# A macaron block on one core: the heads' outputs of three rounds stored and reloaded instead of turned, the preparation reordered, and a new table of ticks

## The chip, the cores and the metric

The kernel runs on one core of a Trainium2 chip. The metric is the device time of one execution in microseconds (us). In the profile PE is TensorE, DVE is VectorE, ACT is ScalarE, POOL is GpSimd and SP is SyncE, which here only issues DMAs.

## What is computed

The input x is 16 batches of 512 rows of 128 numbers. The block is half a feed-forward, attention, half a feed-forward, each added to x:

```python
    x = x + 0.5 * _L0_ffn_ref(_layernorm(x, axis=-1), L0_ffn_weight, L0_ffn_bias)
    x = x + _L0_attn_ref(_layernorm(x, axis=-1), L0_attn_Wq, ..., L0_attn_temperature)
    x = x + 0.5 * _L0_ffn_ref(_layernorm(x, axis=-1), L0_ffn_weight, L0_ffn_bias)
```

The feed-forward is one 128x128 product with a bias, of which both the input and the weight are first rounded to a six-bit grid, with a scale for each block of 32. Attention has 16 heads of 8 dimensions:

```python
        scores = jnp.einsum('bhqd,bhkd->bhqk', Q, K) / scale
        mask = _tpms_mask(L, phase, threshold, temperature)
        scores = scores + TPMS_WEIGHT * jnp.log(mask + 1e-06)[None]
        attn = jax.nn.softmax(scores, axis=-1)
        out = jnp.einsum('bhqk,bhkd->bhqd', attn, V)
        out = out.transpose(0, 2, 1, 3).reshape(B, L, H)
        return out @ Wo + bo
```

The mask depends on the head and not on the batch: a sigmoid of sines and cosines of the two positions.

## The kernel before

Four batches make a **round** (`NQ = 4` rounds of `QB = 4` batches); attention of a round is a **period**. A period is 16 heads, and each head has 8 **ticks** (`STEPS`), two for each batch, so a period has 128 ticks and the kernel 64 heads, numbered m = 0 to 63 here (head 34 is the third head of the third period).

**A tick.** PE makes two blocks of scores (line 1614, 128x512 each) into one of two halves of S_PS; ACT takes the exponential of the 128x1024 result (line 738). In every odd tick PE also makes one of four products of the previous head's exponentials with the values (line 1628, "weighted values"), with a column of ones, so that row 8 of each batch's 32 rows holds the sum. The scores are accumulated on a seed: for the first batch of a head DVE copies the head's logarithmic mask into S_PS (line 1212, four copies of 128x512, the "seeds"). The seeds of a half can only be written when the exponential before has read that half, so between the last exponentials of a head and the first of the next there is a **seam**: exponential of tick 6, two seed copies, scores, exponential of tick 0, and beside it the exponential of tick 7, two more copies, scores of tick 1. A new seed for the later batches is not needed, since the products accumulate differences from one batch to the next.

**The end of a head.** `o_copy` (ACT, line 747) copies O_PS to OTS at the start of the head two later. `turn_o` (PE, line 1637) transposes it in four pieces into R_PS in tick 1, and `o_norm` (DVE, lines 1225 and 1227) divides by the sums and writes the head's 8 columns of AT. After 16 heads the epilogue of the round runs during the next period: for each batch `turn_at` (PE, line 1510), `at_copy` (ACT, line 675), `out_product` (PE, line 1515 with WO), `add_attention` (DVE, 1236), statistics, the rounding to the grid (`centre`, `block_tops`, `block_scales`, `to_grid`, `from_grid`), and per batch `turn_xd1`, `xd_copy1`, `ffn1`, `add_ffn`. The epilogue of the last round stands alone at the end.

**What sets the order.** Each engine's program is written out by hand. `attention(q)` runs through the ticks of a period, and `background(q, tick)` puts the other work (the first feed-forward of later rounds, the chain of projections and splittings into three bfloat16 parts of the next round, the bounds, the epilogue of the previous round) at the ticks that tables name: FIRST, LATE, CHAINS with SECOND, and LAST. In ticks 0 and 1 of a head PE does its background before the tick's scores, in ticks 2 to 7 behind them. In LAST of before the grid of a round is worked in one call over four batches for rounds 0 to 2 and in two calls for the last (`calls_of`).

**The parts of Q and K** are stored in DRAM (q_parts, k_parts) and loaded for each head as a "stack" of six DMAs and a seventh of shift rows (`load_stack`, `load_shift`); the mask of a head is a load of 1 MB (`load_mask`). SP issues all of these in `head(m)`, in program order, in one queue: mask of m+1, stack of m+1, shift of m+1, then stores.

**The preparation** (before the first exponential) makes the sines, the mask of all 16 heads in two halves (`val` on PE, line 1801, 32 tiles; `sigmoid`, line 779, and `ln_mask`, line 786, on ACT), the first feed-forward of round 0, and its projections, with POOL storing the parts. From tile 6 of the first half the factors are stacked three times in the partitions (`COPIES`, `FIRST_COPIED`), and PE waits for those loads.

Of the kernel before, what the change touches and what calls it, by code (L numbers as in the profile page):

```python
# [8 lines left out]
ALU = mybir.AluOpType  # L9
# [20 lines left out]


# [11 lines left out]
K_LOADS = 16 * (2 * len(GROUPS) + 1)  # L43

# [33 lines left out]
FIRST = dict(stats_ve=(0, 2, 4, 8), centre_ve=9, lnexp_act=10, rstd_ve=12, reduce_ve=14, scales_ve=16,  # L78
             to_grid_ve=17, from_grid_ve=19, turn_pe=(22, 24, 28, 32), xd_copy_act=(22, 24, 28, 32),
             ffn_pe=(24, 27, 31, 35), add_ve=(25, 28, 32, 36), stats1_ve=(27, 29, 33, 37), lnexp1_act=(31, 39),  # L80
             rstd1_ve=(33, 41), norm_ve=(41, 57, 73, 89))


LATE = ((dict(stats_ve=(50, 52), lnexp_act=54, rstd_ve=60, centre_ve=64, reduce_ve=66, scales_ve=68, to_grid_ve=72,
              from_grid_ve=74, turn_pe=(82, 90), xd_copy_act=(82, 90), ffn_pe=(84, 92), add_ve=(85, 93),
              stats1_ve=(88, 96), lnexp1_act=98, rstd1_ve=99),
         dict(stats_ve=(82, 83), lnexp_act=87, rstd_ve=91, centre_ve=97, reduce_ve=98, scales_ve=101, to_grid_ve=104,
              from_grid_ve=106, turn_pe=(110, 118), xd_copy_act=(110, 118), ffn_pe=(112, 120), add_ve=(113, 121),
              stats1_ve=(114, 122), lnexp1_act=124, rstd1_ve=125)),
        (dict(stats_ve=(26, 28), lnexp_act=30, rstd_ve=32, centre_ve=33, reduce_ve=34, scales_ve=36, to_grid_ve=41,  # L90
              from_grid_ve=44, turn_pe=(50, 58), xd_copy_act=(50, 58), ffn_pe=(52, 60), add_ve=(53, 61),
              stats1_ve=(57, 66), lnexp1_act=69, rstd1_ve=73),
         dict(stats_ve=(76, 81), lnexp_act=83, rstd_ve=84, centre_ve=90, reduce_ve=91, scales_ve=92, to_grid_ve=97,
# [21 lines left out]
def macaron_kernel(nc, x, Wq, bq, Wk, bk, Wv, bv, Wo, bo, phase, threshold, temperature,  # L115
                   w_ffn, b_ffn, pos, out):
    with ExitStack() as ctx:
# [57 lines left out]
        def stage(h):  # L175
            return big(2048 * STAGE[h], 2048)
# [128 lines left out]
        def first_bank(n, j):  # L305
            return F_PS if n in (2, 3) else (P_PS, F_PS)[j % 2]
# [1585 lines left out]
```

## Time and profile before

| | us |
|---|---|
| median of 3 runs | 877.73 (876.89 to 878.03) |
| the profiled execution: its time | 877.97 |
| the profiled execution: first to last instruction | 876.0 |
| preparation, to the first exponential | 139.0 |
| periods 0, 1, 2, 3 | 179.3, 177.4, 174.0, 160.4 |
| last epilogue | 46.0 |

The profiled execution takes 1.97 us more than its span, and its time is 0.24 us above the median. All stretches are read from the span's start. A period is from the first exponential of its first head to that of the next period; the fourth ends when the last exponentials do.

### The profile page before, as it was taken

How to read it: one execution, taken by the hardware profiler on the slowest of the kernel's cores; microseconds unless marked ns; L12 is line 12 of the kernel's file. 1: busy time of each engine (PE TensorE's matmuls, PEld its weight loads, DVE VectorE, ACT ScalarE, POOL GpSimd, SP SyncE). 2: the span in 40 equal slices, each digit the busy share in tenths (PEclk: the TensorE clock that was granted, in tenths of full speed). 3: DMA queues.
4: the chain of work that ended last, by engine and by line, in shares of the span. 5: the costliest groups of instructions: out<-in, count | busy, mean ns of one | idle time of the engine just before them, and what ended most of it. 6: DMA issues, size and time to landing. Idle time of an engine off the chain costs nothing.

```text
span 876.0 us, 13047 instructions
## 1 busy us (share of the span) xinstructions
PE 738.6 (84%) x4355; PEld 259.7 (30%) x4355; DVE 556.2 (63%) x1464; ACT 669.2 (76%) x799; POOL 191.0 (22%) x164
## 2 busy tenths in 40 slices
PE   0376626999999999999999999999999998999844
PEld 0043311232333323333333234223321331331234
DVE  8866573866889756899784456885433457432265
ACT  1379654888888788888888888888888887888811
POOL 0305750202353203163240031341200002000011
PEclk9987755999999999999999999999999999999987
DMA  5529497865666674756867538668676555456101
GB/s 148 121 77 370 174 314 248 254 209 160 200 207 198 196 222 138 221 185 165 248 191 231 180 114 234 204 170 247 200 225 186 173 173 173 150 192 208 42 1 53
DMA packets 56071, 162.11 MB, mean 185 GB/s; under 512 B 14121, under 2 KB 24497, under 8 KB 45579
## 3 DMA queue, kind: packets, MB, share of 16 engines
q1 hardware_dynamic: 51740, 154.36, 57.4%
q0 software_dynamic: 1808, 5.94, 2.1%
q10 hardware_dynamic: 2446, 0.89, 0.5%
q8 instruction: 37, 0.61, 0.3%
q14 instruction: 40, 0.32, 0.1%
HBM read 117.87 MB, written 43.29 MB: 184 GB/s over the span
## 4 chain that ended last, share of the span: by engine, by line
PE 53%; DVE 20%; ACT 10%; issue 8%; DMA 6%; POOL 2%; SPq 1%; ACTq 0%; DVEq 0%; POOLq 0%
PE S_PS L1614 19%; PE O_PS L1628 18%; ACT BIG L738 9%; DVE S_PS L1212 5%; PE F_PS L1515 4%; PE R_PS L1637 3%; PE F_PS L1510 2%; DMA PART<-trig_parts 2%; DMA k_parts<-PART 2%; PE P_PS L1552 1%; DVE PART L1114 1%; PE P_PS L1515 1%; DVE SC L1053 1%; DVE XC L1098 1%; DVE BIG L1043 1%
## 5 line engine op out<-in xcount | busy, mean ns | idle before, releaser
L738 ACT ACTIVATE BIG<-S_PS 128x1024 f32<-128x1024 f32 x512 | 508.5, 1023 | 109.9 <-PE S_PS L1614 107.6
L1614 PE MATMUL S_PS<-BIG 98*128 98x512 bf16 x1024 | 311.3, 389 | 37.4 <-DMA BIG<-shift_rows 13.7
L1212 DVE COPY S_PS<-BIG 128x512 f32<-128x512 f32 x256 | 159.6, 687 | 180.7 <-ACT BIG L738 178.5
L1628 PE MATMUL O_PS<-BIG,VX 128*9 128x512 f32 x2048 | 268.4, 597 | 1.2 <-ACT OTS L747 1.2
L1614 PEld LDWEIGHTS S_PS<-BIG 98*128 98x128 bf16 x1024 | 79.2, 98 | 290.7 <-ACT BIG L738 136.1
L572 POOL TENSOR_TENSOR XDT<-PART 128x512 bf16<-128x512 f32 x24 | 28.8, 1201 | 292.9 <-ACT PART L706 292.9
L1628 PEld LDWEIGHTS O_PS<-BIG,VX 128*9 128x9 f32 x2048 | 30.8, 88 | 103.4 <-issue 98.7
L549 POOL TENSOR_TENSOR X<-X,BFH 128x512 f32<-128x512 f32 x16 | 24.0, 1521 | 155.2 <-DVE BIG L1043 120.2
L588 POOL TENSOR_TENSOR PART<-PART 128x512 bf16<-128x512 f32 x32 | 41.5, 1297 | 38.5 <-DVE PART L1120 38.5
L581 POOL TENSOR_TENSOR PART<-PART 128x512 f32<-128x512 f32 x32 | 39.6, 1239 | 42.6 <-DVE PART L1114 41.2
L779 ACT ACTIVATE BIG<-S_PS,TEMP 128x1024 f32<-128x1024 f32 x32 | 34.4, 1111 | 18.1 <-PE S_PS L1801 17.6
L549 POOL TENSOR_TENSOR BIG<-BIG,BFH 128x512 f32<-128x512 f32 x16 | 19.9, 1272 | 127.8 <-DVE BIG L1043 111.8
L747 ACT ACTIVATE OTS<-O_PS,CON 128x512 f32<-128x512 f32 x64 | 44.0, 688 | 4.4 <-PE R_PS L1637 4.4
L1637 PE MATMUL R_PS<-IDENT,OTS 128*128 128x128 f32 x256 | 40.3, 280 | 1.8 <-ACT OTS L747 1.8
L675 ACT ACTIVATE XDT<-F_PS 128x512 f32<-128x512 f32 x38 | 22.6, 594 | 18.5 <-PE F_PS L1510 18.5
L1637 PEld LDWEIGHTS R_PS<-IDENT,OTS 128*128 128x128 f32 x256 | 27.7, 142 | 18.2 <-issue 15.0
L1515 PE MATMUL F_PS<-WDT,XDT 128*128 128x128 f32 x208 | 31.0, 295 | 0.0
L1515 PEld LDWEIGHTS F_PS<-WDT,XDT 128*128 128x128 f32 x208 | 27.1, 200 | 12.8 <-ACT XDT L675 7.3
L786 ACT ACTIVATE BIG<-BIG,CON 128x2048 f32<-128x2048 f32 x16 | 30.7, 1987 | 0.0
L1510 PE MATMUL F_PS<-IDENT,BIG 128*128 128x128 f32 x112 | 17.9, 284 | 14.0 <-DVE BIG L1079 10.2
L1114 DVE CAST PART<-PART 128x512 bf16<-128x512 f32 x32 | 22.9, 717 | 10.1 <-ACT PART L706 4.5
L1225 DVE RECIPROCAL RD<-R_PS 128x16 f32<-128x16 f32 x64 | 16.3, 255 | 18.0 <-PE R_PS L1637 17.5
(190 smaller groups left out, 737.8 us busy)
## 6 DMA issues: line engine op xcount, KB each, us to landing
BIG<-ln_masks SPq DMA_DIRECT2D x62, 1024.0 KB, 6.3
ln_masks<-BIG SPq DMA_DIRECT2D x16, 1024.0 KB, 7.1
BIG<-q_parts SPq DMA_DIRECT2D x63, 192.0 KB
BIG<-k_parts SPq DMA_DIRECT2D x63, 144.0 KB
BIG<-q_parts SPq DMA_DIRECT2D x63, 128.0 KB
q_parts<-PART SPq DMA_DIRECT2D x9, 768.0 KB, 3.8
k_parts<-PART SPq DMA_DIRECT2D x18, 384.0 KB, 4.7
BIG<-k_parts SPq DMA_DIRECT2D x63, 96.0 KB
```

What stands on the lines that cost most here:

```text
L549: pool.tensor_tensor(Y, Y, bias[:, None, :].to_broadcast((128, T, H)), ALU.add).then_inc(s[name], 1)
L581: pool.tensor_tensor(F_, F_, hi, ALU.subtract).then_inc(s[f"{q}_r1"], 1)
L588: pool.tensor_tensor(P_[2], F_, P_[1], ALU.subtract).then_inc(s[f"{q}_lo"], 1)
L738: act.activation(E[:, m % 2, j, 2 * pair:2 * pair + 2, :], S_PS[:, pair, :, :], ACT.Exp, scale=LOG_WEIGHT)\
L747: act.activation(OTS[:, :], O_PS[:, :], ACT.Identity, bias=CON[:, 2:3]).then_inc(s["o_copied"], 1)
L779: act.activation(stage(h)[:, 1024 * pair:1024 * pair + 1024].rearrange("p (k l) -> p k l", l=L), S_PS[:, t % 2, :, :], ACT.Sigmoid, scale= ...
L1212: ve.tensor_copy(S_PS[:, pair, i, :], LNM[:, slot, 2 * pair + i, :]).then_inc(s["seeded"], 1)
L1510: mm = pe.transpose(dst[:, 128 * t:128 * t + 128], src[:, t, :], IDENT[:, :])
L1515: mm = pe.matmul(dst[:, 128 * t:128 * t + 128], lhsT[:, 128 * t:128 * t + 128], rhs[:, :], start=True, stop=True)
L1614: mm = pe.matmul(S_PS[:, pair, i, :], KT[0:ALL_ROWS, slot, K_COL[j], 128 * kb:128 * kb + 128], QT[0:ALL_ROWS, slot, j, :], start=False, st ...
L1628: mm = pe.matmul(O_PS[32 * j:32 * j + HD + 1, :], VX[:, slot_of(n), j, kb, h, :], E[:, m % 2, j, kb, :], start=kb == 0, stop=kb == T - 1)
L1637: mm = pe.transpose(R_PS[:, 128 * t:128 * t + 128], OTS[:, 128 * t:128 * t + 128], IDENT[:, :])
```

## The change

- **Outputs by way of DRAM** (rounds 0 to 2, `BY_DRAM = 3`). `turn_o`, `o_norm`, `turn_at` and `at_copy` are left out for heads 0 to 47. SP stores each head's OTS (256 KB) to DRAM (`store_o`, new tensor head_rows), in `head(m)` between the load of the mask and the load of the stack. `o_copy` now waits for the store of the head before (`o_out`) where it waited for the transpose. In the next period the sums of all 16 heads are loaded (`load_sums`), inverted by DVE in one instruction of 128x256 (`invert`), stored and loaded again so that each stands on the 8 partitions of its head (`store_inverses`, `load_inverses`, 1 MB), and the rows are loaded already turned (`load_rows`, 1 MB). DVE multiplies each batch's 128x512 (`normalize`, four for a round), and `out_product` uses that directly. Heads 48 to 63 go the old way.
- **The ticks**: all tables are new. The grid of the epilogue is worked in two calls in every round. More of PE's products stand in ticks 0, 1 and 6.
- **The preparation**: the weight's grid is worked behind the grid of x on DVE, on another tile (WG); PE makes 8 tiles of the mask, then turns the first two batches; tiles up to 11 of the first half are taken with the single copy of the factors (`FIRST_COPIED = (12, 2)`). The parts of odd batches have buffers of their own (QPN_ODD, KP_ODD, in the room of stored masks). POOL adds the output bias of round 0 behind the loads of the first stack. The shift rows of head 0 are copied within SBUF by four small DMAs as soon as they are there; the store to DRAM that they took before follows. On ACT the first bounds stand behind the 11th logarithm instead of the 14th.

The diff, cut to its core:

```diff
+BY_DRAM = NQ - 1
+FIRST_TURNED = NH * BY_DRAM
...
-COPIES, FIRST_COPIED = 3, (6, 2)
+COPIES, FIRST_COPIED = 3, (12, 2)
...
-LAST = ({}, AMID, AMID, ALONE)
+LAST = ({},
+        dict(invert_ve=19, normalize_ve=(42, 45, 50, 57), out_pe=(48, 57, 65, 73), add_ve=(48, 56, 64, 72),
...
+            def store_o(m):
+                n, h = m // NH, head_of(m)
+                sp.wait_ge(s["o_copied"], m + 1)
+                if n >= 2:
+                    sp.wait_ge(s["rows_in"], 16 * (n - 1))
+                sp.dma_start(O_D[n % 2, h].rearrange("r j l -> j r l"), OTS[:, :]).then_inc(s["o_out"], 16)
+
+            def load_sums(n):
+                sp.wait_ge(s["o_out"], 16 * NH * (n + 1))
...
+            def load_rows(n):
+                sp.dma_start(ROWS.rearrange("p j l -> p (j l)"),
+                             O_D[n % 2, :, 0:HD].rearrange("h d j l -> h d (j l)")).then_inc(s["rows_in"], 16)
...
             def head(m):
                 q, i = m // NH, m % NH
                 more = m + 1 < NQ * NH
+                if q > 0:
+                    if i == SUMS_HEAD:
+                        load_sums(q - 1)
+                    if i == SUMS_HEAD + 1:
+                        store_inverses(q - 1)
                 if more and m >= 1:
                     load_mask(m + 1)
+                if q > 0 and i == SUMS_HEAD + 1:
+                    load_rows(q - 1)
+                if q > 0 and i == SUMS_HEAD + 2:
+                    load_inverses(q - 1)
+                if 2 <= m < FIRST_TURNED + 2:
+                    store_o(m - 2)
+                if more and m >= 1:
...
             def o_copy(m):
                 act.wait_ge(s["pv_done"], T * (m + 1))
-                if past(m):
-                    act.wait_ge(s["o_turned"], m)
+                if m > FIRST_TURNED:
+                    act.wait_ge(s["o_turned"], m - FIRST_TURNED)
+                elif past(m):
+                    act.wait_ge(s["o_out"], 16 * m)
...
             pool.wait_ge(s["bound_copied"], 1)
+            for t in range(T):
+                pool.dma_start(QT[QK_ROWS:ALL_ROWS, 0, :, 128 * t:128 * t + 128],
+                               CB4[T * head_of(0) + t:T * head_of(0) + t + 1, :, :, :]).then_inc(s["first_stack"], 16)
             pool.dma_start(SHIFT_D[0].rearrange("e j h (t l) -> (h t) (e j) l", t=T),
                            CB4.rearrange("p e j l -> p (e j) l")).then_inc(s["first_out_shift"], 16)
-            load_shift(pool, 0)
...
+            def normalize(n, j):
+                ve.wait_ge(s["rows_in"], 16 * (n + 1))
+                ve.wait_ge(s["inverse_in"], 16 * (n + 1))
+                TT(ROWS[:, j, :], ROWS[:, j, :], INV[:, j, :], ALU.mult).then_inc(s["at_ready"], 1)
...
-                    if k == 1 and m >= 2:
...
+                    if k == 1 and m >= FIRST_TURNED + 2:
                         turn_o(m - 2)
```

What the change does to the order is seen at three places. The first is PE in head 34 (third head of the third period), here before, from the scores of tick 0 to those of tick 5. S_PS is a score, O_PS the weighted values, R_PS<-IDENT,OTS `turn_o`, F_PS<-IDENT,BIG `turn_at`, F_PS<-WO,XDT `out_product`, the others the chain of the next round:

```order
L1614 MATMUL S_PS<-BIG 128x512 x2
L1637 MATMUL R_PS<-IDENT,OTS 128x128 x4
L1614 MATMUL S_PS<-BIG 128x512 x2
L1628 MATMUL O_PS<-BIG,VX 9x512 x4
L1614 MATMUL S_PS<-BIG 128x512 x2
L1510 MATMUL F_PS<-IDENT,BIG 128x128 x4
L1614 MATMUL S_PS<-BIG 128x512 x2
L1628 MATMUL O_PS<-BIG,VX 9x512 x4
L1614 MATMUL S_PS<-BIG 128x512 x2
L1575 MATMUL R_PS<-XDT,HSEL 16x512
L1515 MATMUL F_PS<-WO,XDT 128x128 x4
L1614 MATMUL S_PS<-BIG 128x512 x2
```

and after, the same ticks (the four score matmuls of ticks 0 and 1 now stand in a row):

```order
L1758 MATMUL S_PS<-BIG 128x512 x4
L1772 MATMUL O_PS<-BIG,VX 9x512 x4
L1758 MATMUL S_PS<-BIG 128x512 x2
L1721 MATMUL R_PS<-XDT,HSEL 16x512
L1758 MATMUL S_PS<-BIG 128x512 x2
L1772 MATMUL O_PS<-BIG,VX 9x512 x4
L1758 MATMUL S_PS<-BIG 128x512 x2
L1729 MATMUL R_PS<-HSEL,XDT 128x16 x4
L1731 MATMUL R_PS<-KDIAG,ONES 128x16
L1758 MATMUL S_PS<-BIG 128x512 x2
```

The transposes of OTS and of AT are gone, and the output product has moved to a later head (four heads later for the first batch), into tick 0 or 1.

The second place is SP in one head of the second half of the third period, before (a mask, then the stack and shift rows of the next head):

```order
L421 DMA BIG<-ln_masks 128x2048
L361 DMA BIG<-k_parts 48x1536
L364 DMA BIG<-q_parts 48x2048
L361 DMA BIG<-k_parts 32x1x1536
L364 DMA BIG<-q_parts 32x1x2048
L361 DMA BIG<-k_parts 16x1x1536
L364 DMA BIG<-q_parts 16x1x2048
L374 DMA BIG<-shift_rows 2x4x512
```

and after:

```order
L430 DMA BIG<-q_parts 48x2048
L427 DMA BIG<-k_parts 32x1x1536
L430 DMA BIG<-q_parts 32x1x2048
L427 DMA BIG<-k_parts 16x1x1536
L430 DMA BIG<-q_parts 16x1x2048
L440 DMA BIG<-shift_rows 2x4x512
L477 DMA shift_rows<-CB 64x2x128
L487 DMA BIG<-ln_masks 128x2048
L495 DMA head_rows<-OTS 4x32x512
```

The store of a head's rows, with an outer size of 4, stands ahead of the stack.

The third is PE at the start of the preparation, before (S_PS is a pair of scores of the mask, P_PS<-IDENT,XC and F_PS<-IDENT,XC turn the first feed-forward's input, WDT is its weight):

```order
L1506 MATMUL P_PS<-IDENT,XC 128x128
L1801 MATMUL S_PS<-PART 128x512 x20
L1510 MATMUL P_PS<-IDENT,XC 128x128 x4
L1510 MATMUL F_PS<-IDENT,XC 128x128 x4
L1801 MATMUL S_PS<-PART 128x512 x2
L1515 MATMUL P_PS<-WDT,XDT 128x128 x4
L1801 MATMUL S_PS<-PART 128x512 x2
L1515 MATMUL F_PS<-WDT,XDT 128x128 x4
```

and after:

```order
L1943 MATMUL S_PS<-PART 128x512 x16
L1656 MATMUL P_PS<-IDENT,XC 128x128 x4
L1656 MATMUL F_PS<-IDENT,XC 128x128 x4
L1943 MATMUL S_PS<-PART 128x512 x4
L1955 MATMUL R_PS<-IDENT,BIG 128x128
L1943 MATMUL S_PS<-PART 128x512 x2
L1661 MATMUL P_PS<-WDT,XDT 128x128 x4
L1661 MATMUL F_PS<-WDT,XDT 128x128 x4
```

The weight is turned behind ten pairs instead of ahead of them, the first two batches behind eight pairs instead of ten, and the two products stand behind eleven.

## Rows read from the trace of the kernel before

**Rows 1.** Busy time by stage: preparation, four periods, last epilogue.
```profile
core 0: us, PE busy (x) PEld busy (x) DVE busy (x) ACT busy (x) POOL busy (x), PEclk, DMA share, GB/s
0.00:139.00 139.00, 57.90 (x212) 29.00 (x213) 94.75 (x296) 75.26 (x64) 51.12 (x52) 0.79 0.61 194
139.00:318.29 179.29, 168.54 (x985) 53.95 (x984) 135.04 (x354) 149.38 (x194) 45.20 (x36) 0.96 0.70 217
318.29:495.67 177.38, 172.33 (x1073) 61.33 (x1073) 128.53 (x348) 151.39 (x195) 46.21 (x36) 1.00 0.66 195
495.67:669.64 173.97, 167.36 (x1025) 55.35 (x1025) 101.25 (x230) 148.19 (x182) 38.47 (x32) 1.00 0.67 198
669.64:830.00 160.36, 151.51 (x926) 44.06 (x926) 70.50 (x156) 138.25 (x154) 4.97 (x4) 0.99 0.52 162
830.00:876.00 46.00, 21.00 (x138) 16.00 (x138) 26.12 (x83) 6.77 (x15) 5.00 (x4) 0.83 0.07 26
```

**Rows 2.** The same view for single heads: 46, 50 and 54.
```profile
650.28:659.96 9.68, 8.94 (x53) 2.00 (x54) 2.92 (x7) 8.44 (x9) 0.00 (x0) 1.00 0.78 237
689.54:699.56 10.02, 9.94 (x65) 3.46 (x65) 5.13 (x18) 8.89 (x10) 0.00 (x0) 1.00 0.57 176
729.14:741.60 12.46, 9.26 (x54) 2.31 (x54) 12.12 (x18) 8.44 (x10) 4.97 (x4) 0.95 0.59 174
```

**Rows 3.** Instructions in time, the seam from head 46 to 47: start, duration, what.
```profile
658.19 2.47 DVE L1212 COPY S_PS<-BIG 128x512 f32<-128x512 f32 x4 [6.72 <-ACT BIG L738]
658.96 0.69 ACT L747 ACTIVATE OTS<-O_PS,CON 128x512 f32<-128x512 f32 x1
...
659.91 0.63 PE L1637 MATMUL R_PS<-IDENT,OTS 128*128 128x128 f32 x4
...
660.37 0.74 PE L1614 MATMUL S_PS<-BIG 98*128 98x512 bf16 x2
```

**Rows 4.** Instructions of PE in time, head 49, tick 7: start, duration, what.
```profile
687.91 1.16 PE L1515 MATMUL F_PS<-WO,XDT 128*128 128x128 f32 x8
688.91 0.60 PE L1614 MATMUL S_PS<-BIG 98*128 98x512 bf16 x2
```

**Rows 5.** Groups by line: busy us, mean ns | idle before; DVE's part of `o_norm`.
```profile
L1227 DVE TENSOR_TENSOR BIG<-R_PS,RD 128x128 f32<-128x128 f32 x64 | 18.6, 291 | 2.2
...
L1225 DVE RECIPROCAL RD<-R_PS 128x16 f32<-128x16 f32 x64 | 16.3, 255 | 18.0 <-PE R_PS L1637 17.5
```

**Rows 6.** Instructions in time in the preparation, idle time before them in brackets.
```profile
43.36 1.89 PE L1801 MATMUL S_PS<-PART 108*128 108x512 bf16 x4 [6.03 <-DMA PART<-trig_parts]
...
48.53 0.69 DVE L1421 COPY XDT<-P_PS 128x512 f32<-128x512 f32 x1 [6.23 <-PE P_PS L1510]
...
85.19 0.88 DVE L1114 CAST PART<-PART 128x512 bf16<-128x512 f32 x1 [4.11 <-DMA q_parts<-PART]
...
121.78 0.42 ACT L719 ACTIVATE Q<-Q 128x256 f32<-128x256 f32 x1 [5.19 <-DVE Q L1181]
...
139.00 1.94 ACT L738 ACTIVATE BIG<-S_PS 128x1024 f32<-128x1024 f32 x2 [12.57 <-PE S_PS L1614]
```

**Rows 7.** Groups by line: the preparation's sigmoids and logarithms on ACT.
```profile
L779 ACT ACTIVATE BIG<-S_PS,TEMP 128x1024 f32<-128x1024 f32 x32 | 34.4, 1111 | 18.1 <-PE S_PS L1801 17.6
...
L786 ACT ACTIVATE BIG<-BIG,CON 128x2048 f32<-128x2048 f32 x16 | 30.7, 1987 | 0.0
```

**Rows 8.** The chain of work that ended last, 129 to 138 us.
```profile
129.13 6.27 DMA shift_rows<-OTS
...
135.69 2.20 DMA BIG<-shift_rows
```

**Rows 9.** DMA issues of the third period: count, KB each, median us to landing.
```profile
BIG<-ln_masks SPq DMA_DIRECT2D x16, 1024.0 KB, 7.1
...
out_dram<-BIG SPq DMA_DIRECT2D x4, 256.0 KB, 4.8
```

**Rows 10.** SP's issues in time: shift rows of head 48, the last of its stack.
```profile
661.21 0.64 SPq L374 DMA_DIRECT2D BIG<-shift_rows  x1
```

More of the change, by code:

```diff
@@ L446, in head @@
                     load_x(2)
-                if q > 0 and i in (11, 12, 13, 14):
-                    store(q - 1, i - 11)
+                if q > 0:
+                    for j, tick in enumerate(LAST[q]["add_ffn_ve"]):
+                        if i == tick // STEPS + 1:
+                            store(q - 1, j)
                 for j, c in enumerate(CHAINS[q]):
@@ L766, in xd_copy1 @@
                 act.wait_ge(s["y_psum"], (n + 1) * QB)
-                if j == 0 and n + 3 < NQ:
-                    act.wait_ge(s["ffn_psum0"], (n + 3) * QB + 2)
+                if n + 3 < NQ:
+                    tick = LAST[n + 1]["xd_copy_act"][j]
+                    act.wait_ge(s["ffn_psum0"], (n + 3) * QB + len([t for t in LATE[n + 1][0]["xd_copy_act"] if t < tick]))
                 if is_short(n) and n == NQ - 1:
@@ L1324, in background @@
                     n = q - 1
+                    if tick == LAST[q]["invert_ve"]:
+                        invert(n)
+                    if tick in LAST[q]["normalize_ve"]:
+                        normalize(n, LAST[q]["normalize_ve"].index(tick))
                     if tick in LAST[q]["add_ve"]:
@@ L1711, in background @@
                     n = q - 1
-                    if tick in LAST[q]["turn_pe"]:
-                        turn_at(n, LAST[q]["turn_pe"].index(tick))
                     if tick in LAST[q]["out_pe"]:
@@ L1803, in val @@
                 mm.then_inc(s["val_ready"], 1)
+            pe.wait_ge(s["trig_in0"], 96)
+            for t in range(8):
+                val(t)
+            turn_xd0(0, 0)
+            turn_xd0(0, 1)
+            val(8)
+            val(9)
+            pe.wait_ge(s["w_grid"], 14)
+            pe.transpose(R_PS[:, 0:H], WG[:, 5, :], IDENT[:, :]).then_inc(s["w_turned"], 1)
+            val(10)
             pe.wait_ge(s["w_grid"], 15)
-            pe.wait_ge(s["trig_in0"], 96)
-            steps = {9: (turn_xd0, 0, 1), 10: (ffn0, 0), 11: (ffn0, 1), 12: (turn_xd0, 2, 3), 13: (ffn0, 2), 14: (ffn0, 3)}
-            for t in range(HALF_TILES):
+            ffn0(0, 0)
+            ffn0(0, 1)
+            steps = {11: (turn_xd0, 2, 3), 12: (ffn0, 2), 13: (ffn0, 3)}
+            for t in range(11, HALF_TILES):
                 if t == FIRST_COPIED[0]:
```

449 lines of the change are left out of this document (258 added, 191 removed).

## The prediction

> **What bounds the kernel now.** I read busy time by stage first [rows 1]. In the three full periods PE is busy 168.5, 172.3 and 167.4 of 179.3, 177.4 and 174.0 us, ACT 149.4, 151.4 and 148.2; the last epilogue is 46.0 us in which nothing is changed; in the preparation no engine is busy above 94.8 of 139.0 us (DVE), so it is a chain of waits. Then single heads [rows 2]. Head 46 has no background at all and takes 9.68 us; 16 such heads are 154.9 us. The periods stand 24.4, 22.5, 19.1 and 5.5 us above that, 71.5 us together. This is all that a better arrangement of the periods can win, and what the empty head costs must be known first.
>
> The seam shows it [rows 3]. DVE starts the four seed copies at 658.19 and ends them at 660.66; the second score of tick 1 can't stand before that. `turn_o` begins at 659.91 and the scores of tick 1 at 660.37, so it takes 0.46 us of PE, and it lies in the time in which PE would wait for the third and fourth seed. **In an empty head its removal gives nothing.** In head 50 a transpose of 0.46 and a product of 1.00 (687.91 to 688.91 [rows 4]) are added, 1.46 us of PE, and the head takes 10.02 us, 0.34 more [rows 2]. So a head hides about 1.1 us of PE's background in the seam, and what is above that lengthens it. The second thing that lengthens heads is DVE in front of the seeds: in head 54 DVE is busy 12.12 of 12.46 us with the grid of four batches in one piece while PE is busy only 9.26 [rows 2].
>
> **The DRAM path on PE and ACT.** Without `turn_o` the seam hides 0.46 us more. That counts only in heads which have more background than they hide, by the tables some 13 heads of period 0, 15 of period 1 and 13 of period 2: 6.0, 6.9 and 6.0 us. In periods 1 to 3 four `turn_at` go as well, 4 x 0.46 = 1.8 us, and four `at_copy` of ACT beside them; I give the pair 2 us a period. `normalize` on DVE (four of 128x512, 0.69 us at most, as four copies of that size take 2.47 [rows 3]) lies where DVE is idle half the time.
>
> **DVE.** It loses 0.255 + 0.291 us a head [rows 5], 46 times, 25 us, of which the most is idle time won; and it gains three inversions of 128x256. No row has that size: the bound from below is 0.26 us (128x16 [rows 5]), from above 4.1 (16 times the columns). I take 2, since most of a small operation is not its columns, and it costs nothing if it keeps off ticks 6 and 7; it stands at ticks 3, 6 and 5 of a head, so up to 2 us a period, which stays in the range. The grid in two calls halves the pieces in front of seeds: head 54 stands 2.8 us above the empty one, and that is what period 3 can lose; I take 1.5 there, 1 in periods 1 and 2 each.
>
> **The ticks.** More products stand in ticks 0, 1 and 6, beside the seam, which rows 2 and 3 show to be the cheap places. I cannot read a price off each move and take nothing for period 0, 1 us for each of the others, with bounds of 8 us lost and 8 us won over all: an operation at tick 3 or 4 goes on the path with its whole length, one at the seam with a quarter (0.34 of 1.46).
>
> Periods: 0: -6. 1: -6.9 - 2 - 1 - 1 = -10.9. 2: -6.0 - 2 - 1 - 1 = -10. 3 (no DRAM path for its own heads but for 48 and 49's turns in place): -2 - 1.5 = -3.5, and a third of that is uncertain. Sum about -30; I take **-28**, from -12 (only `turn_at` and half of the hidden 0.46) to -42 (as above, and the moves worth 8 and DVE's stalls gone). It stays far below the 71.5 us that there are.
>
> **DMA's side.** A head's store is 256 KB; the nearest row is the store of x, the same size, 4.8 us to landing [rows 9]. It is issued when `o_copy` ends, at the start of a head, ahead of the stack of the next head. `o_copy` of the next head comes 9.7 us later (it starts at 658.96 [rows 3], 1 us ahead of the head), so the store has 8.7 us. The stack, whose last issue was 1.2 us into the head (661.21, head 47 began at 659.97) [rows 10], now begins only behind the store: by SP's issues of 0.3 to 0.7 us it ends some 5 us into the head, 4 us ahead of its use. The queue carries 256 KB more a head, an eighth of what it moves, at a DMA share of 0.66 to 0.78 [rows 1, 2]. Masks take 7.1 us to land [rows 9] and are asked for 14 us ahead. So there is room, but some heads will wait: the one with the loads of rows and inverses (2 MB more) in each of three periods, 1 us each. I take **+3**, from 0 to +10.
>
> The Trainium skill ("DMA: Bandwidth & Descriptors", "Why a DMA increments its semaphore by 16 and not by 1") speaks against this store: a DMA is split over as many of the 16 engines as divide the outer sizes of both sides, up to 16, and this one's outer size is 4. On four engines 256 KB takes four times as long as on all; with the page's rate of about 27 GiB/s for an engine that is an estimate of 2.4 us and the page's 2 us for completion, 4.4 in all if those engines are free, and they also carry their share of masks and stacks. By the page the sum would not change, but the landing comes nearer to the 8.7 us. No row here shows a DMA of that form.
>
> **The preparation**, by steps. (a) PE waits 6.03 us for the tripled factors and DVE behind it 6.23 us for the turned batches [rows 6]; now 12 tiles need the single copy, and the turns stand ahead. The grid of x starts where the weight's stood, so the products come some 7 us sooner, and the end of the first half, with what PE still has to do, 5 us sooner (4 to 7). (b) DVE waits 4.11 us for the store of Q's parts [rows 6]; with two buffers it doesn't: 4. What it waits for next is the store of two masks, written long before. (c) The store of shift rows of 6.27 us, then the load of 2.20 [rows 8], becomes four small copies: with 4 issues of 0.6 instead of one, 4.5 saved. (d) Projections are ordered so that PE stands less behind DVE, and ACT's bounds come three logarithms sooner; ACT waits 5.19 us for them now and 12.57 for the first scores [rows 6]. I give this 7, from 0 to 12. Sum 20.5, **-21**. The floor is ACT: 32 sigmoids, 34.4 us, and 16 logarithms, 30.7 [rows 7], from about 30 us on, with table loads about 101 us, against 118 that I forecast. Bounds -12 and -28. Everything that is behind it starts sooner too, so the stores of masks crowd the first heads; up to 3 us, inside the bounds.
>
> **Sum.** 877.97 (the profiled execution's own time, 876.0 and 1.97 around it) - 21 - 28 + 3 = 832; against the median, 0.24 us lower, the same number.
>
> **Rivals.** (1) The forecast, both gains come: 812 to 848. (2) **The periods hardly move**: the freed 0.46 us lies in the seam, as in the empty head, and DVE or the seeds set the heads. For it: DVE is busy 135 us in period 0 and heads like 54 are DVE's; against: PE is busy 97% of period 1, with 1.0 us of hidden room filled. Then -8 in the periods and -18 in the preparation, +3: 855, from 848 to 866. (3) **The store comes too late and `o_copy` waits.** ACT stands at `o_copy` in front of the exponentials of the head, PE behind those, and DVE's seeds behind them. For 46 heads each us of landing above 8.7 costs 46 us. It decides from a landing of 9.7 us: +46 uses up the gain of 46, and above it the kernel is slower: at 10.2 it is 877.97 - 49 + 69 = 898. For it: the store stands behind the remainder of a mask of 7.1 us, masks and stacks share the queue, and the DMA share of an empty head is 0.78 already [rows 2]. Against: 256 KB lands in 4.8 us in the same queue [rows 9], and the queue's gaps leave 2 us a head. That the stack comes late is the same mechanism on PE. The skill's four engines are the form in which it would come. A milder one, 9.2, gives 852. (4) **Better than forecast**: heads fall near to 9.7 to 10 us and the preparation to 112: 800 to 812. (5) The reordering does nothing on the chip, since other waits take the place of those removed in both parts: 876 to 880; nothing in the rows speaks for it, as 6.27 us of a store on the last chain are gone for good.
>
> **How the numbers follow.** (1) 0.62, (2) 0.17, (3) 0.11, of which 0.07 slower and 0.04 between 850 and 875, (4) 0.08, (5) 0.02. Forecast **832**. The range must leave out no more than 2 in 10: 812 leaves out (4), and above, 858 leaves out (5), the worse third of (2) and most of (3): **812 to 858**. A measurement tells about 0.2% (1.8 us) from no change. Faster 0.90, same 0.02, slower 0.08.
>
> **What would show it.** The first exponential near 118 us, no idle time of PE for trig_parts before the first turn, and the last chain without a store of shift rows. No L1637-like transposes before the last period; empty heads still at 9.7 us (if they fall below, my reading of the seam is wrong); heads with background shorter by about 0.5 us; period lengths near 173, 166, 164 and 157. DVE's idle time in front of the seeds ended by ACT. In the DMA issues head_rows landing in 5 to 7 us, and no exponential or `o_copy` of ACT waiting for a DMA on head_rows; if it does, (3). Wrong would be the forecast if the periods keep their lengths while PE's busy time falls.

## The result: 950.6 us, slower

The changed kernel takes a median of 950.55 us (948.79 to 955.59, four runs), the kernel before 877.88 beside it: ratio 1.083, 95% interval 1.080 to 1.085. The forecast was 832, with 812 to 858. The profiled execution has a span of 946.9 us. Where single executions of a kernel fell in the chip's slower state (one of five of `b_4dma`, at 1083 us, and three of eight of `e_hold`), its median below includes them and its ratio leaves them out.

The first six rows are busy time by stage and answer to [rows 1]; the last two are heads 35 and 36 (start and end, length, busy us and count of each engine, granted clock, DMA share, GB/s):
```profile
0.00:136.77 136.77, 63.97 (x212) 31.62 (x213) 108.33 (x296) 74.94 (x64) 52.75 (x55) 0.78 0.61 197
136.77:325.58 188.81, 163.09 (x929) 47.77 (x928) 125.41 (x345) 148.03 (x193) 43.77 (x36) 0.94 0.74 226
325.58:533.24 207.66, 172.22 (x993) 54.97 (x992) 122.00 (x320) 150.34 (x193) 44.02 (x36) 0.92 0.66 196
533.24:731.10 197.86, 163.78 (x945) 47.82 (x944) 94.37 (x212) 146.93 (x180) 38.93 (x32) 0.93 0.70 207
731.10:900.80 169.70, 148.85 (x902) 42.07 (x900) 71.85 (x169) 137.00 (x152) 5.03 (x4) 0.97 0.62 172
900.80:946.90 46.10, 21.09 (x138) 16.09 (x138) 26.13 (x83) 6.75 (x14) 5.00 (x4) 0.83 0.07 25
566.93:586.59 19.66, 10.08 (x56) 2.63 (x55) 4.89 (x12) 9.89 (x13) 2.19 (x2) 0.81 0.99 251
586.59:601.43 14.84, 10.71 (x51) 2.16 (x50) 3.23 (x5) 9.13 (x11) 3.44 (x3) 0.85 0.67 161
```
The preparation gave 2.2 us, not 21. Against [rows 1] the periods lost 9.5, 30.3, 23.9 and 9.3 us, 73 together, and the epilogue is the same. In no period is an engine busier than before by more than 1 us; they wait. Heads 35 and 36 take twice and one and a half times as long as an empty head, at a DMA share of 0.99 and 0.67. PE's granted clock is 0.81 and 0.85 in them, where heads 46 and 50 of [rows 2] have 1.00, so part of what PE does between its waits is slower too.

The waits by line (us in total, times, longest):
```profile
PE S_PS L1758 <- DMA BIG<-shift_rows: 95.9, 35, 9.5
...
ACT OTS L878 <- DMA head_rows<-OTS: 10.5, 7, 3.8
```
The kernel before had 13.7 us of the first, once, in the preparation; here all 35 are in the periods. So PE waits for stacks in 35 places, while `o_copy` on ACT, for whose wait I gave a price, waits little. The chain of work that ended last, heads 35 and 36 (start, duration, what):
```profile
565.90 14.51 DMA head_rows<-OTS
...
580.49 0.70 ACT OTS L878
...
581.21 0.58 SPq L495
...
585.58 14.73 DMA BIG<-shift_rows
...
600.35 1.89 PE S_PS L1758 x4
```
A store of 256 KB takes 14.5 us (the other two on this chain, in the first two periods, take 12.1 and 11.7), `o_copy` waits for it, the next store waits for `o_copy`, the stack stands behind that store on SP, and its last part lands 14.7 us later. At the end of this second landing, in head 36, PE stands idle while the queue works like this (start and end, length, busy us of PE, PEld, DVE, ACT and POOL, granted clock, DMA share, GB/s):
```profile
597.00:600.00 3.00, 0.00 (x0) 0.00 (x0) 1.38 (x3) 0.69 (x1) 2.95 (x3) 0.95 0.26 102
```
A mean share of 0.26 of 16 engines is the work of about four. The issues of the whole execution (count, KB each, median us to landing) show that masks take longer too, and the two new large loads longest:
```profile
BIG<-ln_masks SPq DMA_DIRECT2D x62, 1024.0 KB, 9.3
...
head_rows<-OTS SPq DMA_DIRECT2D x48, 256.0 KB
...
BIG<-head_rows SPq DMA_DIRECT2D x3, 1024.0 KB, 12.8
BIG<-inverse_sums SPq DMA_DIRECT2D x3, 1024.0 KB, 19.0
```

### The profile page after: what moved, and what is told of

It reads as the page before. It is cut to its first block, busy times and chain, and to the rows that moved or that the text cites. A ratio compares the mean times of both kernels' runs of the same rounds, so it can differ in the third digit from the quotient of the medians.

```text
span 946.9 us, 12520 instructions
## 1 busy us (share of the span) xinstructions
PE 733.0 (77%) x4115; PEld 240.3 (25%) x4115; DVE 548.1 (58%) x1425; ACT 664.0 (70%) x793; POOL 189.5 (20%) x167
## 3 DMA queue, kind: packets, MB, share of 16 engines
q1 hardware_dynamic: 59804, 174.02, 61.4%
## 4 chain that ended last, share of the span: by engine, by line
PE 33%; DMA 26%; DVE 12%; ACT 10%; SPq 10%; issue 7%; POOL 1%; DVEq 0%; POOLq 0%; ACTq 0%
DMA BIG<-shift_rows 21%; PE S_PS L1758 13%; PE O_PS L1772 11%; ACT BIG L867 7%; SPq L427 4%; SPq L430 4%; DMA head_rows<-OTS 4%; PE F_PS L1661 3%; DVE S_PS L1320 2%; ACT OTS L878 1%; PE P_PS L1661 1%; DVE ST L1045 1%; DMA BIG<-OTS 1%; PE F_PS L1656 1%; SPq L495 1%
## 5 line engine op out<-in xcount | busy, mean ns | idle before, releaser
L1758 PE MATMUL S_PS<-BIG 98*128 98x512 bf16 x1024 | 313.8, 403 | 128.8 <-DMA BIG<-shift_rows 95.9
L1772 PE MATMUL O_PS<-BIG,VX 128*9 128x512 f32 x2048 | 279.0, 619 | 1.2 <-ACT OTS L878 1.2
L878 ACT ACTIVATE OTS<-O_PS,CON 128x512 f32<-128x512 f32 x64 | 44.0, 687 | 14.9 <-DMA head_rows<-OTS 10.5
L704 POOL TENSOR_TENSOR PART<-PART 128x512 bf16<-128x512 f32 x28 | 36.9, 1317 | 63.8 <-DVE PART L1228 63.8
L1943 PE MATMUL S_PS<-PART 36*128 36x512 bf16 (+1 forms) x32 | 14.7, 575 | 30.0 <-DMA PART<-trig_parts 27.9
L697 POOL TENSOR_TENSOR PART<-PART 128x512 f32<-128x512 f32 x28 | 33.8, 1207 | 20.1 <-DVE PART L1222 17.6
L1661 PEld LDWEIGHTS F_PS<-WDT,XDT 128*128 128x128 f32 x160 | 23.7, 218 | 5.6 <-issue 3.3
L1661 PE MATMUL F_PS<-WDT,XDT 128*128 128x128 f32 x160 | 24.9, 306 | 0.0
L800 ACT ACTIVATE XDT<-F_PS 128x512 f32<-128x512 f32 x20 | 11.9, 596 | 18.1 <-PE F_PS L1656 17.8
L794 ACT ACTIVATE RS<-VE 128x8 f32<-128x8 f32 (+1 forms) x22 | 4.5, 206 | 26.0 <-DVE VE L1052 18.7
L1252 DVE TENSOR_REDUCE KTOP<-R_PS 16x1 f32<-16x512 f32 x12 | 8.1, 677 | 24.6 <-PE R_PS L1721 24.5
L1045 DVE BATCH_NORM_STATS2 ST<-X 128x6 f32<-128x128 f32 x96 | 20.9, 280 | 0.6
```

Of the source, the lines that this page charges most:

```text
L697: pool.tensor_tensor(F_, F_, hi, ALU.subtract).then_inc(s[f"{q}_r1"], 1)
L704: pool.tensor_tensor(P_[2], F_, P_[1], ALU.subtract).then_inc(s[f"{q}_lo"], 1)
L878: act.activation(OTS[:, :], O_PS[:, :], ACT.Identity, bias=CON[:, 2:3]).then_inc(s["o_copied"], 1)
L1661: mm = pe.matmul(dst[:, 128 * t:128 * t + 128], lhsT[:, 128 * t:128 * t + 128], rhs[:, :], start=True, stop=True)
L1758: mm = pe.matmul(S_PS[:, pair, i, :], KT[0:ALL_ROWS, slot, K_COL[j], 128 * kb:128 * kb + 128], QT[0:ALL_ROWS, slot, j, :], start=False, st ...
L1772: mm = pe.matmul(O_PS[32 * j:32 * j + HD + 1, :], VX[:, slot_of(n), j, kb, h, :], E[:, m % 2, j, kb, :], start=kb == 0, stop=kb == T - 1)
```

## Experiments

There are three theories of the loss. **A** is the order: the stack is issued late, since the store ahead of it waits for `o_copied`. **B** is the form: a store of 4 groups of 32 rows sits on few DMA engines and clogs them. **C** is the two 1 MB loads of rows and inverses, ahead of stacks in heads 3 and 4 of a period. Ratios are against the kernel before, run beside each group on the same chip (877.1 to 879.3 us).

### Order and form, in the changed kernel

Store behind the stack (`e_order`):
```diff
-                if 2 <= m < FIRST_TURNED + 2:
-                    store_o(m - 2)
                 if more and m >= 1:
...
                     if i < NH - 1:
                         load_shift(sp, m + 1)
+                if 2 <= m < FIRST_TURNED + 2:
+                    store_o(m - 2)
```


> The changed kernel with one thing altered: the store of a head's output is issued behind the stack and shift rows of the next head, not ahead of them. No byte is added or taken away. Theory A (order: the wait for o_copied stands ahead of the stack on SP, so the stack begins 3 to 4 us later in the head than in the kernel before): PE's wait for shift_rows falls from 95.9 us to under 30 in the periods, they come to 180 us or less each, and the time falls to 870 to 895 us. Theory B (the landings themselves are long, because a store of 256 KB whose outer size is 4 and the 2 MB of rows and inverses clog the queue): the stacks of heads 3 and 4 of a period still wait, and the time stays above 925 us.

Measured 926.23 us, ratio 1.056 (1.051 to 1.060).

Store of 128 rows (`e_16eng`):
```diff
-        O_D = nc.dram_tensor("head_rows", [2, NH, 128 // QB, QB, L], F32).ap()
+        O_D = nc.dram_tensor("head_rows", [2, NH, QB, 128 // QB, L], F32).ap()
...
-                sp.dma_start(O_D[n % 2, h].rearrange("r j l -> j r l"), OTS[:, :]).then_inc(s["o_out"], 16)
+                sp.dma_start(O_D[n % 2, h].rearrange("j r l -> (j r) l"), OTS[:, :]).then_inc(s["o_out"], 16)
...
-                sp.dma_start(ROWS.rearrange("p j l -> p (j l)"),
-                             O_D[n % 2, :, 0:HD].rearrange("h d j l -> h d (j l)")).then_inc(s["rows_in"], 16)
+                for j in range(QB):
+                    sp.dma_start(ROWS[:, j, :], O_D[n % 2, :, j, 0:HD]).then_inc(s["rows_in"], 16)
```


> The changed kernel, the store in its old place ahead of the stack, but the outputs lie in DRAM by batch and then by row, so that the store is one of 128 rows of 2 KB and not of 4 groups of 32; the load of rows becomes four of 256 KB. The bytes are the same. Theory B (a store of outer size 4 sits on few DMA engines, and everything behind it on those engines is late): head_rows lands in under 6 us in the heads without other large loads (7.4 to 14.5 in the changed kernel), the long heads 3 and 4 shrink, and the time falls below 915 us. Theory A (order): the time stays above 930 us.

Measured **875.66** us, ratio 0.998 (0.995 to 1.002): 75 us less. The rows' place in DRAM changed with the form, and the load of rows became four; the next section takes the form by itself.

Both edits together (`e_order_16`):

> Both edits together: 128 rows instead of 4 groups, and the store behind the stack. If A and B both hold and add up, PE's wait for shift_rows is nearly only that of the preparation (some 16 us) and the time is 850 to 870 us. If A alone is the cause it is no better than the order alone by more than 3 us; if B alone is, no better than the 128 rows alone.

Measured 872.56, ratio 0.995 (0.991 to 0.998).

The waits of the store behind the stack, and then those and the issues of the kernel with 128 rows:
```profile
ACT OTS L878 <- DMA head_rows<-OTS: 70.4, 25, 8.3
...
PE S_PS L1758 <- DMA BIG<-shift_rows: 35.6, 13, 6.5
```
```profile
PE S_PS L1758 <- DMA BIG<-shift_rows: 32.0, 16, 5.1
```
```profile
BIG<-ln_masks SPq DMA_DIRECT2D x62, 1024.0 KB, 6.6
...
head_rows<-OTS SPq DMA_DIRECT2D x48, 256.0 KB, 5.1
```
With four groups the order moves the wait from PE (95.9 to 35.6) to `o_copy` (10.5 to 70.4), and 24 of 73 us come back, so with this form of the store the order does matter. With 128 rows PE's wait is 32.0 with the store in its old place, masks land in 6.6 us, and the order is worth 3 us, which is inside the intervals of the two runs.

### Each alone, in the kernel before

The wait alone (`b_late`), one line ahead of `load_stack(sp, m + 1)`: `sp.wait_ge(s["o_copied"], m - 1)`.

> The kernel before, with SP made to wait, ahead of the next head's stack, until the output of the head before last is copied, as the store of the changed kernel makes it wait. No DMA is added. This is the lateness alone. Theory A: most of the 73 us lost in the periods comes back: 915 to 940 us. Theory B: the stack begins some 3 us later but lands in time in most heads: 878 to 895 us.

Measured 878.31, ratio 0.999 (0.997 to 1.002). **The wait by itself costs nothing**, and theory A alone is false: PE's wait for shift rows is the 13.7 us of the preparation, as before. It shows nothing on a wait that a late store has made longer; that is the 24 us of `e_order`.

The store alone, with `o_copy` made to wait for it, as 4 groups (`b_store4`), as 128 rows (`b_store16`), and as four DMAs of 32 rows to the same addresses as the 4 groups (`b_4dma`):
```diff
+            def store_o(m):
+                n, h = m // NH, head_of(m)
+                sp.wait_ge(s["o_copied"], m + 1)
+                for j in range(QB):
+                    sp.dma_start(O_D[n % 2, h, :, j, :], OTS[32 * j:32 * j + 32, :]).then_inc(s["o_out"], 16)
```


> The kernel before with nothing but the store of a head's output added, as the changed kernel has it: 4 groups of 32 rows, ahead of the stack, with ACT's copy waiting for it, in the 48 heads of the first three periods. Nothing reads what is stored; the turns by PE stay. Theory B (the form of the store alone makes the loss): 920 to 955 us, with masks landing in 9 us instead of 6, and period 3, which has two such stores, unchanged at 160. If the loss needs the changed kernel's ticks or its loads of rows and inverses: 880 to 895.

Measured 932.12 (926.08 and 938.17, two runs), ratio 1.062 (1.045 to 1.079).

> The same, with the store as 128 rows of 2 KB. The same 256 KB a head go to the same queue at the same point. Theory B: 878 to 886 us, the price of 12 MB in gaps of the queue. If it is the bytes that cost and not their form, it is as slow as its twin with 4 groups.

Measured 878.63, ratio 1.001 (0.999 to 1.002).

> The kernel before with the store added as in the kernel that took 932 us: the same point, the same bytes, the same addresses in DRAM (by row, then by batch), but as four DMAs of 32 rows each and not as one of 4 groups of 32 rows. SP issues three DMAs more a head, ahead of the stack. If the loss comes from how one DMA of outer size 4 is spread over the engines, this is as fast as 128 rows: 878 to 886 us. If it comes from where the rows go in DRAM (pieces of 2 KB at steps of 8 KB), it stays above 910.

Measured 881.70, ratio 1.004 (1.001 to 1.006).

So 12 MB more in the queue are free, the addresses in DRAM and three more issues a head cost 3 us together, and the same bytes to the same addresses as one DMA of 4 groups cost 54 (40 to 69 by the interval). Masks, whose median to landing is 5.7 us with 128 rows, take 9.0 with 4 groups. The queue's row (packets, MB, share of 16 engines) of the kernel with 4 groups, then that row and the store's landing of the one with 128 rows:
```profile
q1 hardware_dynamic: 58076, 166.94, 58.1%
```
```profile
q1 hardware_dynamic: 58652, 166.95, 59.3%
...
head_rows<-OTS SPq DMA_DIRECT2D x48, 256.0 KB, 3.8
```
The mean over 16 engines is the same (lower, even, in the kernel with 4 groups, whose span is longer). The mean hides the few: this kernel too has stretches in which about four engines' worth of work is left, from 196 to 200 us at a share of 0.26 and 98 GB/s, while the one with 128 rows has stretches in which the queue is empty (193 to 195 us, share 0.00).

### The two large loads

`e_split`, on top of 128 rows and the order: rows by batch in heads 2 and 3, inverses in heads 4, 5 and 6, all behind the stack; `normalize` of a batch waits for its own two loads.
```diff
+ROWS_AT, INV_AT = {2: (0, 1), 3: (2, 3)}, {4: (0, 1), 5: (2,), 6: (3,)}
...
+                if q > 0:
+                    load_rows(q - 1, ROWS_AT.get(i, ()))
+                    if i in INV_AT:
+                        load_inverses(q - 1, INV_AT[i])
```


> The changed kernel with 128 rows and the store behind the stack, and the 2 MB of rows and inverses no longer in two blocks ahead of the stacks of heads 3 and 4: by batch, 256 KB each, behind the stack, rows in heads 2 and 3, inverses in heads 4, 5 and 6. Theory C (what is left of the loss is these two blocks: heads 3, 4 and 5 of periods 1 to 3 stand 25 us together above 10.4 us each): the time is 847 to 856 us and PE's wait for shift_rows falls from 28 us to the preparation's. If these heads are long because of their ticks: 868 to 873.

Measured **853.26** (847.81 to 858.71, two runs), ratio 0.972 (0.957 to 0.987). Heads 35 and 36 without the split, then with it:
```profile
517.99:533.61 15.62, 10.28 (x56) 2.90 (x57) 6.34 (x16) 10.00 (x14) 2.19 (x2) 0.93 0.98 280
533.61:548.80 15.19, 11.40 (x52) 2.23 (x50) 3.23 (x5) 9.03 (x10) 3.44 (x3) 0.84 0.90 202
```
```profile
511.13:522.78 11.65, 10.42 (x57) 2.78 (x57) 5.89 (x15) 9.90 (x14) 1.04 (x1) 1.00 0.90 255
522.78:532.74 9.96, 8.79 (x50) 2.04 (x50) 3.25 (x7) 8.91 (x11) 2.07 (x2) 1.00 1.00 275
```
Theory C holds for what B leaves, about 19 us. Period 0, which has no such loads, is unchanged (172.8 and 172.6 us), and periods 1 to 3 are 19 us shorter together. Whether it is the smaller pieces or their place behind the stacks was not separated. PE's wait for shift rows fell to 15.7 us in 13 places, 2.6 at most, where the expectation had none in the periods. With two runs 11 us apart this kernel alone does not settle the size of the gain over the kernel before; the next two do.

Fewer bytes on top of that, 112 rows (`f_112`) or only the 9 of each batch that are read (`f_9`, four DMAs of `OTS[32 * j:32 * j + HD + 1, :]`):

> The split kernel (853 us), with the store cut from 128 rows to the first 112, which hold all that is read. 32 KB less a head, of some 1.9 MB. If the queue's load sets the waits that are left (PE 15.7 us for shift rows, ACT 12.4 us for head_rows), 850 to 853 us; if not, no difference: 853.

Measured **852.15** (848.10 to 853.78), ratio 0.969 (0.965 to 0.972).

> The split kernel, with the store cut to the 9 rows of each batch that are read: four DMAs of 18 KB, 72 KB a head and not 256. SP issues three more a head, behind the stack. If the queue's load sets the waits that are left, this gains more than 112 rows do: 845 to 851 us, and ACT's wait for head_rows is gone. If SP's issues are what is scarce, it loses 2 to 5 us: 855 to 858.

Measured **851.14** (848.50 to 854.42), ratio 0.968 (0.965 to 0.971). The two are the same within their intervals, and both beat the kernel before and the changed one. The 184 KB less a head bring nothing that can be told in time. ACT's wait for head_rows was expected to be gone with 9 rows; it rose, from 7.1 us with 112 rows to 15.9, while PE's for shift rows went from 8.7 to 7.2. So fewer bytes and three more issues may offset each other.

### The preparation

`e_hold`, on 128 rows and the order, stores masks 9 to 12 behind the first stack's landing:

> The changed kernel with 128 rows and the store behind the stack; in the preparation the stores of masks 9 to 12 (4 MB) are issued only when the first stack has landed, not at 114 to 121 us, where they lie in the queue beside the last store of K's parts (6 us) and the first stack and its shift rows (9 us). Theory P (the preparation's last chain is lengthened by its own mask stores): the first exponential comes at 127 to 131 us instead of 136.6, head 1 grows by 1 to 3 us, and the time is 865 to 869. Otherwise, if four small copies take 9 us by themselves: 136 us as now.

Measured 876.87, ratio 0.996 (0.993 to 0.998), against 0.995 of its twin (`e_order_16`): the same time. The first exponential came at 128.5 us, 8.1 sooner, as expected; head 1 took 18.5 us instead of 11.0:
```profile
139.86:158.39 18.53, 9.56 (x47) 1.60 (x40) 15.35 (x19) 8.54 (x11) 4.96 (x4) 0.68 1.01 314
```
The 4 MB then stand in head 1 (DMA share 1.01), and period 0 grew by 13.5 us. With half of it held (`f_9_hold2`, on the kernel with 9 rows):

> The kernel with 9 rows, and masks 11 and 12 stored only when the first stack has landed; 9 and 10 stay where they are. With all four held the first exponential came 8 us sooner and period 0 took 13.5 us longer, since head 1 waited for them. If half of it keeps the gain without the loss: first exponential at 132 us, head 1 at 11 to 12 us, 3 to 4 us faster than its twin. If the queue's work is only moved: within 2 us of it.

Measured 856.86, ratio 0.974 (0.971 to 0.978): 5.7 us slower than its twin: the first exponential came at 131.0, 4.0 us sooner, head 1 took 14.7 us instead of 11.6, and period 0 grew by 4.4. So the queue's work was only moved. A further 4.2 us stand in period 3 (161.3 against 157.1), far behind the held stores; the kernels with split loads, whose fourth periods have nearly the same program, show 156.9 to 161.3 us there, so that part I take for scatter.

`p_lnexp` moves ACT's second logarithm of the statistics (`if i in (0, 5)`), `p_dram` takes the first shift rows by DRAM again; both on 112 rows:

> The kernel with 112 rows (852 us), with ACT's second statistics logarithm behind five mask logarithms and not behind two. In the changed kernel ACT stands 5.96 us there, waiting for DVE. If ACT's chain sets the end of the preparation, its last mask is ready up to 6 us sooner and the first exponential comes at 131 to 133 us: 847 to 850. If DVE's and POOL's chain of the projections sets it, the later logarithm delays batches 2 and 3 or changes nothing: 852 to 856.

Measured 853.47, ratio 0.972 (0.968 to 0.976). The first exponential came 2.7 us sooner, at 132.9. The periods are 3.4 us longer together, 3.7 of them in period 2, so no gain can be told; that the earlier start caused the loss is not shown.

> The kernel with 112 rows, with the first head's shift rows stored to DRAM and loaded from there, as in the kernel before, and not copied by four small DMAs. The forecast gave the copies 4.5 us. If that holds, the first exponential is 4 to 5 us later than 135.6 and the time 856 to 857. If the queue, full of mask stores at that point, sets the landing either way, 851 to 853.

Measured 849.08 (847.39 to 854.91), ratio 0.969 (0.964 to 0.974). The first exponential is at 135.5, as with the copies. The chain of this kernel:
```profile
121.78 10.15 DMA shift_rows<-OTS
...
132.21 2.16 DMA BIG<-shift_rows
```
The store takes 10.15 us here and not the 6.27 of [rows 8]. Between 115 and 130 us the DMA share is 1.0 in both kernels (the four mask stores), and the last landing comes at 134.4 and 134.5 us.

### The ticks

The chains' old ticks in the kernel with 112 rows (`t_chains`):

> The kernel with 112 rows, with the tables that set the ticks of the projections' chains (CHAINS, CLOSE, APART) as they are in the kernel before; the ticks of the other preparation and of the epilogues stay as changed. Forecast: the moves are worth 1 us a period, so 853 to 856. If the 17 to 20 us that the periods gained are the work of the ticks and not of the transposes taken off PE: 862 to 870.

Measured **870.42**, ratio 0.990 (0.986 to 0.993), 18 us slower than its twin. Stages of the kernel with 112 rows, then the periods with the chains' old ticks:
```profile
0.00:135.58 135.58, 58.35 (x212) 28.00 (x213) 108.26 (x296) 75.17 (x64) 52.81 (x55) 0.82 0.62 198
135.58:307.01 171.43, 160.33 (x929) 47.37 (x928) 125.63 (x331) 148.28 (x194) 44.07 (x36) 0.96 0.79 245
307.01:477.48 170.47, 162.59 (x992) 53.34 (x990) 122.78 (x330) 149.43 (x192) 44.09 (x36) 0.99 0.81 240
477.48:645.37 167.89, 158.39 (x944) 47.90 (x944) 95.99 (x217) 146.07 (x181) 39.67 (x32) 0.99 0.79 240
645.37:804.65 159.28, 148.35 (x902) 42.25 (x902) 72.43 (x171) 137.35 (x152) 5.04 (x4) 0.99 0.61 182
```
```profile
136.85:318.85 182.00, 166.49 (x928) 49.05 (x926) 127.02 (x326) 148.89 (x193) 46.48 (x36) 0.94 0.75 232
318.85:494.26 175.41, 165.26 (x992) 51.82 (x992) 128.00 (x335) 148.94 (x192) 46.01 (x36) 1.00 0.77 232
494.26:668.55 174.29, 161.18 (x944) 46.41 (x944) 97.30 (x217) 145.85 (x180) 39.71 (x32) 0.99 0.76 232
668.55:825.41 156.86, 146.83 (x902) 41.80 (x902) 72.37 (x171) 137.25 (x152) 5.04 (x4) 1.00 0.60 184
```
By these two executions the chains' ticks are worth 10.6, 4.9 and 6.4 us in periods 0 to 2, and cost 2.4 in period 3, which has no chains; that I take for the same scatter. Period 1 by itself proves little: the kernels with split loads and the new chains have 168.6 to 175.5 us there (`p_dram`, `f_9_hold2`). The 18 us of the whole are clear of the intervals. A caution: old chains beside new other ticks make head 13 of period 0 last 16.4 us, 11.0 in the kernel before; some 5 us of the 10.6 are that mismatch. The tables of the other preparation (LATE) were not put back, since the order of accesses to a PSUM bank rests on them.

## Why the prediction was wrong

**The step that failed is the term "+3 DMA's side", from 0 to +10.** It was worth some 97: 75 for the form of the store (950.55 to 875.66; in the kernel before the form alone costs 54) and some 22 for the loads and the order (875.66 to 853.26). Three things were wrong in it.

- *A mean instead of the fullest engines.* I set 256 KB against "an eighth of what it moves" at a share of 0.66 to 0.78. These shares are means over 16 engines. An estimate: from the queue's row of the changed kernel (174.02 MB at 61.4% of 16 engines over 946.9 us) an engine moves 18.7 GB/s when busy, so 64 KB on each of four (the 0.26 above) are 3.5 us a head, on top of a mean of 0.66 to 0.70 of 11 us [rows 1], 7.5: 11.0 of 11 us are full, and what is late is hardly made good. With the 24 GB/s an engine of a stretch at 390 GB/s it would be 10.2 of 11. The bytes and shares for this sum stood in the trace of before; that four engines carry the store did not. The nearest row that I priced the store with [rows 9] was one of the same bytes and another form; it bounds nothing for a DMA on fewer engines.
- *What is behind it.* I asked when the store itself must land (8.7 us) and not what else runs on those engines. Masks and stacks do: the masks' median landing went from 6.3 to 9.3 us, and PE waited in 35 places for stacks that had been in time. The point from which rival 3 was to decide, a landing of 9.7 us, was passed by the three stores on the chain (11.7 to 14.5 us), and 950 lies above the 898 of that rival too; but the loss came mostly by PE's stack (95.9 us of waits, against 10.5 at `o_copy`), which I had put down as "the same mechanism" without a price.
- *Two 1 MB loads in front of stacks.* I gave one head a period 1 us for both. Heads 35 and 36 took 15.6 and 15.2 us with the store repaired, and 11.7 and 10.0 with the loads split and moved: 9 us in one period.

The Trainium skill ("DMA: Bandwidth & Descriptors", "Why a DMA increments its semaphore by 16 and not by 1") has the rule by which four engines carry this store, and the prediction cited it and then wrote that "the sum would not change". The pair of 932 and 879 us agrees with the rule, and so do four DMAs of 32 rows (882) and the share of 0.26. By the same section of the Trainium skill a DMA on HWDGE takes always the lowest-numbered engines, and the stack's DMAs, with an outer size of 8 in DRAM, would lie on the lower eight, the store's four among them; no run here shows which engines they are.

The sums of the prediction hold but for small ones: 64 KB at the rate that it took from the Trainium skill are 2.3 us and not 2.4, and what the range leaves out by the prediction's own chances is 0.23 or more, not 0.2. The slower outcome had 0.08.

**What held.** The stack "now begins only behind the store" and ends "4 us ahead of its use": as long as the store isn't late itself this costs nothing (`b_late`, 878.3). "In an empty head its removal gives nothing": head 47 of the kernel with 9 rows, without a transpose, takes 9.68 us, as in [rows 2], and so do heads 48 to 52; only head 46 is shorter, 8.9, behind a head 45 that is longer:
```profile
639.53:649.21 9.68, 8.53 (x48) 1.62 (x48) 2.48 (x5) 8.44 (x9) 0.00 (x0) 1.00 0.76 230
```
With the DMAs repaired the kernel gains 27 us (852.15 against 879.27 beside it), not 46.

**The periods, -28.** With 112 rows they are 7.9, 6.9, 6.1 and 1.1 us shorter than [rows 1], 22 together; forecast 6, 10.9, 10 and 3.5. The size is near, the reasons were not: I gave the transposes off PE 6 to 7 us a period and the moved ticks nothing to 1. With the old ticks of the chains the periods are 2.5 us shorter than [rows 1] all together, or some 8 if head 13's mismatch is taken out; this holds the DRAM path and the epilogue's new tables together, and the chains' ticks made the rest. The step that failed is "I cannot read a price off each move and take nothing". The step beside it, 13 to 15 heads times 0.46 us, probably counted hidden work as path; no run has the new ticks with the transposes still on PE, so the price of the transposes there stays open.

**The preparation, -21, measured 2.2 (3.4 with 112 rows).** ACT in the changed kernel (start, duration, what, idle before it), and the chain behind the last store of K's parts:
```profile
69.25 0.21 ACT L794 ACTIVATE RS<-VE 128x8 f32<-128x8 f32 x1 [5.96 <-DVE VE L1052]
...
105.37 5.23 ACT L911 ACTIVATE BIG<-S_PS,TEMP 128x1024 f32<-128x1024 f32 x5 [3.68 <-PE S_PS L1943]
...
136.77 1.02 ACT L867 ACTIVATE BIG<-S_PS 128x1024 f32<-128x1024 f32 x1 [8.83 <-PE S_PS L1758]
```
```profile
115.94 4.99 DMA k_parts<-BIG
...
126.41 9.24 DMA BIG<-OTS
```
(a), 5 us: PE's wait of 6.03 [rows 6] is gone, but the first half's sigmoids end only 0.8 us sooner, since PE now waits 1.51 us for the weight's grid on DVE, and ACT up to 3.71 for PE, which has the products in between. (b), 4 us: came; the last store of parts is issued 3.5 us sooner. (c), 4.5 us: the copies take 9.24 us where store and load took 6.27 + 0.28 + 2.20 [rows 8]; their landing is set by the queue, and `p_dram` shows no difference. (d), 7 us: did not come; ACT has new waits (5.96, 3.68) and its last logarithm ends at 127.9 us, 1.5 later than before, so no exponential could have begun at 118. Behind all of it stands what I named in half a sentence, "the stores of masks crowd the first heads": `e_hold` took 8 us off the preparation and paid 13.5 in period 0, and `f_9_hold2` took 4.0 off and paid 4.4. What a preparation without that queue would give was not measured.

## What to carry to other kernels

A DMA's price has three parts: bytes, the number of engines that carry it, and what else stands on those engines; set the last against the fullest engine and not against the mean share. Here 256 KB with 128 rows outermost on both sides, or four pieces with 32, did no harm, and 4 groups on one side did; look at the outermost dimension before anything else is tuned around the transfer. Loads that are not urgent go behind those that are, in pieces that fit a head's gap. And time gained by holding back stores for a queue that is full was paid back here as soon as the queue had to carry them.

## What the runs showed of the hardware

- The same 256 KB from SBUF to DRAM, in the kernel before: as 128 rows a median of 3.8 us to landing, and masks land in 5.7; as four DMAs of 32 rows 2.7 us each, masks 5.9, and 3 us of time in 48 heads; as 4 groups of 32 rows masks 9.0 and 54 us. For the 4 groups themselves the profile gives no median; the three on the changed kernel's chain took 11.7 to 14.5 us.
- While PE waited for the end of a stack in the changed kernel the DMA share was 0.26 at 102 GB/s (597 to 600 us): about four of 16 engines, 25 GB/s each.
- A broadcast of 16 rows of 8 KB to 128 partitions (1 MB) landed in 19.0 us, the load of rows of the same size in 12.8, and the core's DMA share was 0.99 at only 251 GB/s in head 35, in which both were under way, against 1.00 at 390 GB/s while masks were stored from 115 to 120 us (`e_order_16`). The share is the time that packets took, so for the same bytes they took half as long again. Why is open.
- Heads 35 and 36, in which PE waited for stacks, show a granted clock of 0.81 and 0.85 (mean 0.91 over the execution, 0.948 before), so part of the loss is PE's own work at the lower of its two levels: 10.71 us in head 36 against 8.79 in the same head of the split kernel, at 1.00.
